# A transformer tower with an expert layer on one core: where small weights, zero rows and a slot table are made, and in which order the middle stage issues its parts

## The chip, the cores and the metric

One Trainium2 chip, one core of it. The time is the device time of one execution, in microseconds (us); the figure for a kernel is the median of its runs. A core has five engines that run their own instruction streams and meet at semaphores: PE (TensorE, matrix products), DVE (VectorE), ACT (ScalarE), POOL (GpSimd) and SP (SyncE, which here only issues DMAs). A stream is executed strictly in order, so an instruction that waits holds up all that stands behind it on its engine. That goes for the queue of DMAs that an engine issues as well.

## The reference

The input is 128 images of 2x104x104. They become 128 x 169 = 21,632 tokens of 128 numbers (a patch embedding over five shifted copies of the image). Four residual blocks follow:

```python
h = _L0_tok_ref(x, gamma, beta, W, b)                       # patch embedding
h = h + _L0_attn_ref(_layernorm(h), positions, scales, ...)  # attention to 256 learned positions
h = h + _L0_ffn_ref(_layernorm(h), weight)                   # quantised product 128x128
h = h + _L1_attn_ref(_layernorm(h))                          # softmax(x x^T) x within an image
h = h + _L1_ffn_ref(_layernorm(h), ...)                      # 64 experts, six a token
```

The last one routes every token to six of 64 experts, adds a shared expert of all tokens, and has a capacity per expert of C = int(N * 6 * 2 / 64) rows:

```python
router_probs = softmax(x @ router_w.T + bias);  topk_p, topk_i = top_k(router_probs, 6)
slot = pos - group_starts                      # place of a pair within its expert
expert_in[e, slot] = x[token]                  # scatter
expert_out = (silu(expert_in @ w_gate.T) * (expert_in @ w_up.T)) @ w_down.T
sparse = segment_sum(gate * expert_out, token) # back to the tokens, six rows each
out = shared_out + sparse
```

## The kernel before

The program has three stages.

**Front** (to about 648 us): embedding and first attention, image positions in 43 groups of four. The change leaves it alone.

**Middle**: 64 blocks of two images (the b parts: quantised product and second attention) and 43 groups of four tiles of 128 tokens (the r parts: shared expert, routing, slots). All five engines walk through the same steps, in which a function `braid` (line 130) puts the parts. A part `('b', 1, scores)` stands in step s for block s-1; an r part has its group by `place_of(r) = LATE + 3*(r//2) + 2*(r%2)` (line 125), with LATE = 5. So from step 5 on, two steps of three carry an r group and the third has b parts alone. The order of the parts within a step is the order in the list, one list for each engine:

- PE (lines 1374 to 1377): shared_up, turn_q, ffn, turn_x, scores, count, shared_down, mix, turn_r, route.
- ACT (line 1495): tanh, norm_q, root_x, root_r, copy_q, copy_x, probs, expo, copy_x4.
- DVE (line 1837): ffn_out, silu_gate, quant, stats_r, root_x, root_r, norm_x, attn_out, choose, silu_up, place, denominator, norm, shared_out.

One block's chain is norm_q (ACT, L1415 and L1420), quant (DVE, L1522 to L1532), turn_q (PE, L1213), copy_q (ACT, L1391), ffn (PE, L1220), ffn_out (DVE, L1538, L1504, L1509), root_x (ACT L1428, then DVE L1516), norm_x (DVE, L1546), turn_x (PE, L1228), copy_x (ACT, L1398), scores (PE, L1238), expo (ACT, L1408), mix (PE, L1249), attn_out (DVE, L1555, L1561). One group's chain is stats_r, root_r (L1435, L1573), norm (L1580), turn_r (L1257), copy_x4 (L1452), route (L1268, L1271), then in the next r step tanh (L1459), silu_gate (L1616), shared_up (L1278), choose (L1593 to L1610), probs (L1466, L1471), silu_up (L1624), count (L1290, L1293), place (L1631 to L1652), denominator (L1660 to L1673), shared_down, shared_out (L1683).

POOL has one part, `scatter` (lines 1075 to 1090): after place and denominator of a group it issues 24 indirect DMAs, one for each tile and each of the six choices, which write 128 rows of `xr` into the list of the experts' rows `xed`. Behind each stands a one-column memset of `pace`, for which the next one waits.

SP issues load_h1, store_h3, store_h4 and load_h3 by the same steps. ACT's queue issues seven loads before its first step (lines 1437 to 1446): the router's and the shared expert's weights (rwt, sgu, sdt, rbias), the experts' weights for all 64 experts in two DMAs (wgu, 4096 KB, and wdt, 2048 KB), and the zero rows behind `xed`. The slot table `first` (the number of each expert's first row) is made in three steps: DVE writes a diagonal `diag`, PE multiplies ones by it (first_rows, line 1338, behind PE's parts of step 2), DVE copies the product (line 1715, in constants(), ahead of its parts of step 3).

After the middle, DVE and PE build tables of tiles (`tab_ready`). Then comes the **expert stage**: 270 steps q of four tiles. SP loads four row tiles (`xin<-xed`, L1150) whose numbers it reads from the table; PE turns and multiplies; ACT writes the weighted rows `yo` (L1491); POOL's `spread` (lines 1092 to 1103) issues four indirect DMAs a step, which write them to `ytk`, by token and choice. SP's DMAs that zero the ends of the experts' lists (lines 1180 to 1185) stand as one block between the loads of step q = 7 and q = 8. From q = 218 on a function `weave` adds one `add_up` (lines 1848 to 1871) in every second step, until 26 groups are done: SP loads 128x4x6 rows of 128 (`yg<-ytk`), DVE adds the six of each token, the first of its additions in one instruction on 128x1536 (L1856). Groups 26 to 31 follow behind the last step; the last eleven (32 to 42) wait until all spreads have landed.

## Time and profile before

| | us |
|---|---|
| median of three runs (lowest to highest) | 3638.26 (3630.31 to 3639.31) |
| the profiled execution | 3652.29 |
| its span in the trace | 3650.5 |
| front, to the first instructions of the middle | 648 |
| first scatter to last scatter on POOL | 785.6 to 2130.8 |
| spreads on POOL | 2131.1 to 3582.9 |
| from there to the end of the span | 67.6 |

Busy shares of the whole span are PE 72%, DVE 62%, ACT 44%, POOL 76%. A share over the span mixes the stages. The row of POOL in forty slices shows it at 8 and 9 tenths from slice 9 to slice 39. The other engines' rows stand well under theirs there. The granted TensorE clock is low (5 and 6 tenths of full speed) in the middle stage and 7 to 8 tenths in most of the expert stage. Register and branch instructions and the issuing of DMAs do not count as busy.

### The profile page before, as it was taken

The page shows a single profiled execution, that of the slowest core. Times are in us where ns is not written, and L with a number is a line of the kernel's source. Part 1 is how long each engine was busy: PE and PEld are TensorE (multiplying, and loading weights), DVE is VectorE, ACT ScalarE, POOL GpSimd, SP SyncE. Part 2 cuts the span into 40 slices and gives each one's busy share as a digit, 9 for nine tenths or more (in the row PEclk, how much of TensorE's full clock was granted, in tenths as well). Part 3 has the DMA queues.
Part 4 walks back from the last instruction along what each step waited for, and adds up shares of the span by engine and source line. Part 5 has one row for each costly group of instructions (what it writes and reads, how often), then busy time and mean ns, then how long its engine had stood idle before and what let it go on. Part 6 is the DMA issues. An engine that isn't in the chain of part 4 may idle for free. (4 is left out here: it accounts for less than half of the span.)

```text
span 3650.5 us, 70832 instructions
## 1 busy us (share of the span) xinstructions
PE 2639.7 (72%) x14073; PEld 1949.1 (53%) x14074; DVE 2248.0 (62%) x7707; ACT 1602.5 (44%) x4279; POOL 2765.1 (76%) x4608
## 2 busy tenths in 40 slices
PE   5888987477776777777677446777778888877770
PEld 4777775244443444444344245656667677667660
DVE  6999998466666667666666534444444444457665
ACT  4888887344443444444443123333333333333320
POOL 4777773038888888888888868888888888888882
PEclk7999998556656555655656569888887777777765
DMA  7777773313232222222222154334333333369768
GB/s 274 245 241 241 240 244 131 92 47 98 86 96 88 93 89 83 90 75 84 75 79 70 58 143 117 108 109 111 107 109 111 108 107 101 104 207 283 235 220 299
DMA packets 387802, 501.76 MB, mean 137 GB/s; under 512 B 68888, under 2 KB 319889, under 8 KB 376178
## 3 DMA queue, kind: packets, MB, share of 16 engines
q1 hardware_dynamic: 303458, 366.96, 33.3%
q0 software_dynamic: 83232, 126.60, 10.4%
q10 hardware_dynamic: 944, 6.63, 0.6%
q14 instruction: 144, 1.18, 0.1%
q8 instruction: 24, 0.39, 0.0%
HBM read 257.02 MB, written 264.08 MB: 143 GB/s over the span
## 5 line engine op out<-in xcount | busy, mean ns | idle before, releaser
L1097 POOL DMA_INDIRECT ytk<-yo,idxy x1080 | 1084.9, 1005 | 243.6 <-POOL pace L1103 204.1
L1085 POOL DMA_INDIRECT xed<-xr,idxs x1014 | 1002.9, 989 | 334.8 <-POOL pace L1090 176.2
L1491 ACT ACTIVATE yo<-wide,gi 128x128 f32<-128x128 f32 x1080 | 308.7, 368 | 894.1 <-DMA ytk<-yo,idxy 854.8
L1825 DVE SCALAR_TENSOR_TENSOR ae<-the,bank 128x256 f32<-128x256 f32 x270 | 113.5, 421 | 693.6 <-ACT the L1482 686.1
L1316 PE MATMUL bank<-wgu,xeT 128*128 x2160 | 392.5, 339 | 174.9 <-ACT xeT L1476 158.1
L1316 PEld LDWEIGHTS bank<-wgu,xeT 128*128 128x128 f32 x2160 | 347.0, 244 | 228.8 <-issue 228.1
L1334 PE MATMUL wide<-wdt,hT 64*128 x2160 | 373.4, 322 | 123.1 <-DVE hT L1834 121.5
L1334 PEld LDWEIGHTS wide<-wdt,hT 64*128 64x128 f32 x2160 | 312.8, 220 | 175.7 <-issue 173.0
L586 POOL TENSOR_TENSOR weff<-w,gam 128x384 f32<-128x384 f32 x338 | 305.4, 938 | 9.1 <-DMA tokb<-in_tokb 9.1
L1249 PE MATMUL wide<-xn,e 128*128 128x128 f32 (+3 forms) x1024 | 251.9, 366 | 43.2 <-ACT e L1408 43.2
L1306 PE MATMUL bank<-ident,xin 128*128 128x128 f32 x1080 | 214.1, 334 | 46.8 <-DMA xin<-xed 46.8
L1238 PE MATMUL bank<-xnT 128*128 128x169 f32 (+1 forms) x512 | 206.5, 532 | 41.9 <-ACT xnT L1398 41.9
L597 POOL TENSOR_TENSOR big<-big,scb 128x1024 f32<-128x1024 f32 (+1 forms) x43 | 103.9, 2416 | 171.7 <-ACT big L729 171.7
L1249 PEld LDWEIGHTS wide<-xn,e 128*128 128x128 f32 (+3 forms) x1024 | 144.3, 187 | 149.4 <-issue 74.1
L1325 PE MATMUL wide<-ident,hh 128*64 128x128 f32 x1080 | 217.5, 337 | 0.0
L1476 ACT ACTIVATE xeT<-bank 128x512 f32<-128x512 f32 x270 | 165.8, 614 | 85.8 <-PE bank L1306 85.7
L618 PE MATMUL bank<-weff,xs 128*128 128x128 f32 x1690 | 200.5, 279 | 0.8 <-POOL weff L586 0.8
L1306 PEld LDWEIGHTS bank<-ident,xin 128*128 128x128 f32 x1080 | 171.1, 177 | 53.1 <-issue 47.3
L618 PEld LDWEIGHTS bank<-weff,xs 128*128 128x128 f32 x1690 | 196.5, 196 | 2.6 <-issue 2.6
L1834 DVE COPY hT<-wide 64x512 f32<-64x512 f32 x270 | 182.6, 676 | 16.9 <-PE wide L1325 15.5
L1452 ACT ACTIVATE x4T<-wide 128x512 f32<-128x512 f32 (+1 forms) x43 | 25.4, 590 | 313.4 <-PE wide L1257 313.4
L1238 PEld LDWEIGHTS bank<-xnT 128*128 128x128 f32 (+1 forms) x512 | 91.7, 237 | 129.5 <-issue 113.0
(324 smaller groups left out, 5428.9 us busy)
## 6 DMA issues: line engine op xcount, KB each, us to landing
xin<-xed SPq DMA_DIRECT2D x1080, 74.0 KB
ytk<-zeros SPq DMA_DIRECT2D x42, 1536.0 KB, 9.6
yg<-ytk SPq DMA_DIRECT2D x42, 1536.0 KB
xs<-in_xcol SPq DMA_DIRECT2D x42, 1280.0 KB, 6.7
ytk<-yo,idxy POOLq DMA_INDIRECT x1080
xed<-xr,idxs POOLq DMA_INDIRECT x1014
H<-in_ximg SPq DMA_DIRECT2D x4, 2704.0 KB, 19.2
h1d<-H SPq DMA_DIRECT2D x42, 256.0 KB, 9.0
```

Of the source, the lines that this page charges most:

```text
L586: ins = p.tensor_tensor(weff[:, slot, j, k0:k1, :], w5[:, k0:k1, :], gam[:, bass.ds(TG * g + j, 1), k0:k1].rearrange("p o c -> p (o c)").u ...
L618: pe.matmul(psY[slot][:, j * D:(j + 1) * D], xs[:, slot, j, k, :], weff[:, slot, j, k, :], start=(j == 0 and k == 0), stop=False)
L1085: p.indirect_dma_start(xed[:, :], bass.IndirectOffsetOnAxis(ap=idxs[:, slot, j, k:k + 1], axis=0), xr[:, slot, j, :], None, bounds_check=Z ...
L1097: p.indirect_dma_start(ytk[:, :], bass.IndirectOffsetOnAxis(ap=idxy[:, slot, j:j + 1], axis=0), yo[:, slot % ES, j, :], None, bounds_check ...
L1238: last = pe.matmul(dst, xnT[:, i, 128 * h:128 * h + m], xnT[:, i, 0:T], start=True, stop=True)
L1249: last = pe.matmul(pP[0:m, 256 * i + D * h:256 * i + D * h + D], e[0:m2, i, 128 * h:128 * h + m], xn[0:m2, slot, 2 * i + h2_, :], start=(h ...
L1306: last = pe.transpose(eT_[slot % 2][:, j * 128:(j + 1) * 128], xin[:, slot, j, 0:D], ident[:, :])
L1316: last = pe.matmul(eG[slot % 2][:, j * 128:(j + 1) * 128], xeT[:, slot % 2, j, :], wgu[:, bass.ds(e, 1), :].rearrange("p o f -> p (o f)"), ...
L1325: last = pe.transpose(eH[slot % 2][0:F, j * 128:(j + 1) * 128], hh[:, slot % 2, j, :], ident[:, :])
L1334: last = pe.matmul(eO[slot % 2][:, j * D:(j + 1) * D], hT[:, slot % 2, j, :], wdt[:, bass.ds(e, 1), :].rearrange("p o f -> p (o f)"), star ...
L1491: last = a.activation(yo[:, slot % ES, j, :], eO[slot % 2][:, j * D:(j + 1) * D], ACT.Copy, scale=gi[:, slot, j, 0:1])
L1834: v.tensor_copy(hT[:, slot % 2, :, :].rearrange("p j d -> p (j d)"), eH[slot % 2][0:F, :])\
```

## The change

Four items and a new order of the middle stage.

1. The seven loads leave ACT's queue. SP issues load_h1 of blocks 0 and 1 first, then the small weights and the zero rows, and then its braid from step 2. The experts' weights come expert by expert: load_weights stands in the braid with lag 2 and issues two DMAs a block (64 KB and 32 KB). PE waits for all of them at the head of the expert stage.
2. The slot table comes from a POOL iota (1 + CR * e, the same in every partition) and one DVE copy. `diag`, first_rows and DVE's wait for it are gone, and PE's braid is one piece.
3. The DMA that zeroes an expert's tail is a part of the steps q = 8 to 71, one in each, behind the four row loads of that step.
4. The first addition of add_up is four instructions on 128x384 in place of one on 128x1536.
5. Order. Each engine's list of the middle stage changes. PE: turn_x moves ahead of turn_q, scores ahead of ffn. ACT: root_x goes first, copy_x moves ahead of root_r and copy_q. DVE: root_x, norm_x and attn_out move ahead of quant. One of the two PSUM places of turn_x moves from bank 0 to bank 3.

```diff
-    pX = (bank[0][:, 256:256 + T], bank[2][:, 2 * T:3 * T])
+    pX = (bank[3][:, 2 * T:3 * T], bank[2][:, 2 * T:3 * T])
...
+            p.iota(firsti[:, :], [[CR, NE]], base=1, channel_multiplier=0)
...
-            braid(sp, 0, place_of(GR + 2, LATE) + 1, LATE,
-                  [('b', 0, load_h1), ('b', 3, store_h3), ('r', 3, halves(store_h4)), ('r', 0, load_h3)], 0, GR)
+            def load_weights(g, slot, rnd):
+                sp.dma_start(wgu[:, bass.ds(g, 1), :], io["wgu"][:, bass.ds(g, 1), :]).then_inc(n["s_wt"], 16)
+                sp.dma_start(wdt[:, bass.ds(g, 1), :], io["wdt"][:, bass.ds(g, 1), :]).then_inc(n["s_wt"], 16)
+
+            load_h1(0, 0, 0)
+            load_h1(1, 1, 0)
+            for dst, src in ((rwt, io["rwt"]), (sgu, io["sgu"]), (sdt, io["sdt"])):
+                sp.dma_start(dst[:, :], src).then_inc(n["s_ws"], 16)
...
+            braid(sp, 2, place_of(GR + 2, LATE) + 1, LATE,
+                  [('b', 0, load_h1), ('b', 2, load_weights), ('b', 3, store_h3), ('r', 3, halves(store_h4)), ('r', 0, load_h3)], 0, GR)
...
-            for e in range(0, NE, 4):
-                for row in entries(SP, ttail, e, 4, ZR - 128):
-                    sp.dma_start(xed[bass.ds(row, 128), :], zrow[:, :]).then_inc(n["tail_z"], 16)
-            pipeline(sp, 0, NQ, rows, ES, begin=2 * ES, end=Q0)
+            def zero_tail(q, slot, rnd):
+                row, = entries(SP, ttail, q - 2 * ES, 1, ZR - 128)
+                sp.dma_start(xed[bass.ds(row, 128), :], zrow[:, :]).then_inc(n["tail_z"], 16)
+
+            pipeline(sp, 0, NQ, rows + [(0, zero_tail)], ES, begin=2 * ES, end=2 * ES + NE)
+            pipeline(sp, 0, NQ, rows, ES, begin=2 * ES + NE, end=Q0)
...
-            def first_rows():
-
-                pe.wait_ge(n["first_v"], 1)
-                pe.matmul(rB[:, 0:NE], ones[0:NE, :], diag[:, :], start=True, stop=True).then_inc(n["first_p"], 1)
...
-            parts = [('r', 1, halves(shared_up)), ('b', 0, turn_q), ('b', 0, ffn), ('b', 1, turn_x),
-                               ('b', 1, scores), ('r', 1, halves(count)), ('r', 1, halves(shared_down)), ('b', 1, mix),
+            parts = [('r', 1, halves(shared_up)), ('b', 1, turn_x), ('b', 0, turn_q), ('b', 1, scores),
+                               ('b', 0, ffn), ('r', 1, halves(count)), ('r', 1, halves(shared_down)), ('b', 1, mix),
                                ('r', 0, turn_r), ('r', 0, halves(route))]
...
-            a.wait_ge(h1_in[0], 32)
-            a.wait_ge(h1_in[1], 32)
-            a.dma_start(rwt[:, :], io["rwt"]).then_inc(n["s_ws"], 16)
...
-            braid(a, 0, WHOLE[1], LATE, [('r', 1, halves(tanh)), ('b', 0, norm_q), ('b', 1, root_x), ('r', 0, root_r), ('b', 0, copy_q),
-                              ('b', 1, copy_x), ('r', 1, probs), ('b', 1, expo), ('r', 0, halves(copy_x4))], 0, GR)
+            braid(a, 0, WHOLE[1], LATE, [('b', 1, root_x), ('r', 1, halves(tanh)), ('b', 0, norm_q), ('b', 1, copy_x), ('r', 0, root_r),
+                              ('b', 0, copy_q), ('r', 1, probs), ('b', 1, expo), ('r', 0, halves(copy_x4))], 0, GR)
...
-                v.tensor_scalar(diag[:, :], ident[0:C, 0:C], col[0:C, 10:11], None, ALU.mult).then_inc(n["first_v"], 1)
-                v.wait_ge(n["first_p"], 1)
-                link(v.tensor_copy(first1[:, :], rB[:, 0:NE]))
+                link(v.tensor_copy(first1[:, :], firsti[:, :]))
...
-            order = [('b', 1, ffn_out), ('r', 1, halves(silu_gate)), ('b', 0, quant), ('r', 0, stats_r), ('b', 1, root_x),
-                     ('r', 0, root_r), ('b', 1, norm_x), ('b', 2, attn_out), ('r', 1, choose), ('r', 1, halves(silu_up)),
+            order = [('b', 1, ffn_out), ('b', 1, root_x), ('b', 1, norm_x), ('r', 1, halves(silu_gate)), ('b', 2, attn_out),
+                     ('b', 0, quant), ('r', 0, stats_r), ('r', 0, root_r), ('r', 1, choose), ('r', 1, halves(silu_up)),
...
-                v.tensor_tensor(y[:, :, 0:3, :], y[:, :, 0:3, :], y[:, :, 3:6, :], ALU.add).then_inc(n["add1_r"], 1)
+                for j in range(nj):
+                    last = v.tensor_tensor(y[:, j, 0:3, :], y[:, j, 0:3, :], y[:, j, 3:6, :], ALU.add)
+                last.then_inc(n["add1_r"], 1)
```

In the program's order the change shows at three places. The first is ACT in a step with an r group. `th` is tanh's result, `mrs` and `xq` are norm_q's, `sdb` root_x's, `sdc` root_r's, `xqT` copy_q's, `xnT` copy_x's, `ex` that of probs. ACT_TABLE_LOAD fetches the table of the function that follows it. Before:

```order
L1459 ACTIVATE th<-wide 128x512
L1415 ACTIVATE mrs<-mur 128x8
L1420 ACTIVATE xq<-h1s,mrs 128x128 x4
L1428 ACT_TABLE_LOAD
L1428 ACTIVATE sdb<-mvc,eps_ln 128x4
L1435 ACTIVATE sdc<-mvd,eps_ln 128x4
L1391 ACTIVATE xqT<-bank 128x512
L1398 ACTIVATE xnT<-bank 128x169 x2
L1466 ACT_TABLE_LOAD
L1466 ACTIVATE ex,zz<-lo,top 128x64 x4
```

After, the same step (its lines are some four to seven lower or higher):

```order
L1435 ACT_TABLE_LOAD
L1435 ACTIVATE sdb<-mvc,eps_ln 128x4
L1455 ACT_TABLE_LOAD
L1455 ACTIVATE th<-wide 128x512
L1422 ACTIVATE mrs<-mur 128x8
L1427 ACTIVATE xq<-h1s,mrs 128x128 x4
L1405 ACTIVATE xnT<-bank 128x169 x2
L1442 ACT_TABLE_LOAD
L1442 ACTIVATE sdc<-mvd,eps_ln 128x4
L1398 ACTIVATE xqT<-bank 128x512
L1462 ACT_TABLE_LOAD
L1462 ACTIVATE ex,zz<-lo,top 128x64 x4
```

root_x went ahead of tanh and copy_x ahead of root_r, and the step has four table loads where it had two.

The second is DVE in the same step, from ffn_out's last instruction on. `xn` is norm_x's result, `sa` silu_gate's, `h` attn_out's in the rows with `rzb`, `xq` and `qmag` are quant's. Before:

```order
L1509 BN_AGGR mvc<-bstc 128x2 x4
L1616 SCALAR_TENSOR_TENSOR sa<-th,wide 128x512
L1522 TENSOR_SCALAR xq<-xq 128x512
L1524 TENSOR_SCALAR qmag<-xq 128x512
L1527 TENSOR_SCALAR qmag<-qmag 128x512
L1529 TENSOR_TENSOR xq<-xq,qmag 128x512
L1532 TENSOR_TENSOR xqb<-xq,qmag 128x512
L1504 BN_STATS bstd<-h3s 128x6 x4
L1509 BN_AGGR mvd<-bstd 128x2 x4
L1516 RECIPROCAL rb<-sdb 128x4
L1573 RECIPROCAL rc<-sdc 128x4
L1546 TENSOR_SCALAR xn<-h,mvc,rb 128x128 x4
```

After:

```order
L1505 BN_AGGR mvc<-bstc 128x2 x4
L1512 RECIPROCAL rb<-sdb 128x4
L1542 TENSOR_SCALAR xn<-h,mvc,rb 128x128 x4
L1612 SCALAR_TENSOR_TENSOR sa<-th,wide 128x512
L1551 RECIPROCAL rzb<-zsum 128x2
L1551 RECIPROCAL rzb<-zsum 41x2
L1557 SCALAR_TENSOR_TENSOR h<-wide,rzb,h 128x128
L1557 SCALAR_TENSOR_TENSOR h<-wide,rzb,h 41x128
L1557 SCALAR_TENSOR_TENSOR h<-wide,rzb,h 128x128
L1557 SCALAR_TENSOR_TENSOR h<-wide,rzb,h 41x128
L1518 TENSOR_SCALAR xq<-xq 128x512
```

The root and norm_x went ahead of silu_gate, attn_out ahead of quant.

The third is SP at the start of the middle stage, where `h1s` is what load_h1 fills. Before:

```order
L1113 DMA h1s<-h1d 128x2x128
L1114 DMA h1s<-h1d 41x2x128
L1113 DMA h1s<-h1d 128x2x128
L1114 DMA h1s<-h1d 41x2x128
L1113 DMA h1s<-h1d 128x2x128
L1114 DMA h1s<-h1d 41x2x128
```

After:

```order
L1151 DMA rbias<-in_rbias 128x64
L1153 DMA xed<-zrow 128x148
L1114 DMA h1s<-h1d 128x2x128
L1115 DMA h1s<-h1d 41x2x128
L1144 DMA wgu<-in_wgu 128x128
L1145 DMA wdt<-in_wdt 64x128
L1114 DMA h1s<-h1d 128x2x128
L1115 DMA h1s<-h1d 41x2x128
L1144 DMA wgu<-in_wgu 128x128
L1145 DMA wdt<-in_wdt 64x128
```

The small loads stand between those of block 1 and block 2, and each block's load is followed by the two for one expert's weights.

## Rows read from the trace of the kernel before

**Rows 1.** The page: busy time in forty slices, in tenths.

```profile
POOL 4777773038888888888888868888888888888882
```

**Rows 2.** Groups by line on POOL, 785.5 to 2131 us: busy, mean ns, idle before.

```profile
L1085 POOL DMA_INDIRECT xed<-xr,idxs x1014 | 1002.9, 989 | 334.8 <-POOL pace L1090 176.2 <-issue 145.8 <-DVE xr L1673 3.5
L1090 POOL MEMSET pace<- 128x1 f32 x1014 | 150.7, 149 | 0.0
```

**Rows 3.** The page, the group of the spreads, same columns.

```profile
L1097 POOL DMA_INDIRECT ytk<-yo,idxy x1080 | 1084.9, 1005 | 243.6 <-POOL pace L1103 204.1
```

**Rows 4.** Timeline of POOL at the first scatter: start, length, idle before it.

```profile
785.59 1.31 POOL L1085 DMA_INDIRECT xed<-xr,idxs  x1 [125.29 <-issue]
```

**Rows 5.** Waits of POOL, 785.5 to 2131 us: total, times, longest.

```profile
POOL xed L1085 <- DVE xr L1673: 3.5, 3, 1.4
```

**Rows 6.** Timeline of ACT at the head of the middle stage.

```profile
656.30 0.40 ACTq L1439 DMA_DIRECT2D rwt<-in_rwt  x1
...
659.89 0.21 ACT L1415 ACTIVATE mrs<-mur 128x8 f32<-128x8 f32 x1 [21.50 <-issue]
```

**Rows 7.** Waits of ACT, 640 to 790 us, and of DVE, 660 to 790 us.

```profile
ACT mrs L1415 <- DMA h1s<-h1d: 4.7, 1, 4.7
...
DVE first L1715 <- PE wide L1341: 10.0, 1, 10.0
```

**Rows 8.** Timeline of DVE, 1228 to 1358 us, single rows.

```profile
1228.98 0.17 DVE L1673 SCALAR_TENSOR_TENSOR xr<-e,rden 128x24 f32<-128x24 f32 x1
...
1236.75 0.69 DVE L1616 SCALAR_TENSOR_TENSOR sa<-th,wide 128x512 f32<-128x512 f32 x1 [3.92 <-issue]
...
1243.37 1.14 DVE L1546 TENSOR_SCALAR xn<-h,mvc,rb 128x128 f32<-128x128 f32 x4
...
1244.67 1.12 DVE L1561 SCALAR_TENSOR_TENSOR h<-wide,rzb,h 128x128 f32<-128x128 f32 x4
...
1251.08 0.42 DVE L1631 TENSOR_TENSOR slotm<-wide,taken 128x256 f32<-128x256 f32 x1 [2.33 <-PE wide L1293]
...
1357.17 0.17 DVE L1673 SCALAR_TENSOR_TENSOR xr<-e,rden 128x24 f32<-128x24 f32 x1
```

**Rows 9.** Timeline of ACT in and behind the same step.

```profile
1231.59 0.60 ACT L1452 ACTIVATE x4T<-wide 128x512 f32<-128x512 f32 x1 [7.13 <-PE wide L1257]
...
1238.46 1.28 ACT L1428 ACT_TABLE_LOAD   x1
1239.75 0.30 ACT L1428 ACTIVATE sdb<-mvc,eps_ln 128x4 f32<-128x4 f32 x1
...
1271.76 1.28 ACT L1408 ACT_TABLE_LOAD   x1 [3.46 <-PE bank L1238]
```

**Rows 10.** Timelines of POOL and SP around the only large gap.

```profile
2175.00 0.97 POOL L1097 DMA_INDIRECT ytk<-yo,idxy  x1 [17.87 <-issue]
...
2123.76 3.36 SPq L1185 DMA_DIRECT2D xed<-zrow  x6
...
2164.52 1.93 SPq L1150 DMA_DIRECT2D xin<-xed  x4
```

**Rows 11.** Timelines of POOL and DVE at two of the 32 additions beside spreads.

```profile
3274.84 2.03 POOL L1097 DMA_INDIRECT ytk<-yo,idxy  x1 [0.19 <-POOL pace L1103]
...
3286.17 2.49 POOL L1097 DMA_INDIRECT ytk<-yo,idxy  x1 [0.19 <-POOL pace L1103]
...
3274.27 1.75 DVE L1856 TENSOR_TENSOR yg<-yg 128x1536 f32<-128x1536 f32 x1
...
3286.05 1.76 DVE L1856 TENSOR_TENSOR yg<-yg 128x1536 f32<-128x1536 f32 x1
```

**Rows 12.** Timeline of DVE at the end; its waits, 3583 to 3650 us.

```profile
3643.27 1.76 DVE L1856 TENSOR_TENSOR yg<-yg 128x1536 f32<-128x1536 f32 x1 [2.38 <-DMA yg<-ytk]
...
3647.06 0.55 DVE L1856 TENSOR_TENSOR yg<-yg 128x384 f32<-128x384 f32 x1
...
DVE yg L1856 <- DMA yg<-ytk: 25.6, 10, 9.0
```

21 lines of the change are left out of this document (7 added, 14 removed).

## The prediction

> **What bounds the kernel now.** I read the busy rows in forty slices first [rows 1]: POOL stands at 8 or 9 tenths from slice 9 to slice 39, and no other engine does. Then POOL's groups. The 1014 scatters take 1002.9 us, their memsets 150.7, and the idle time ahead of them is 334.8, of which 125.3 lie before the first one [rows 2, 4]. The rest is the 0.2 us behind each memset, and some 20 us of "issue" in eight short pieces, where the loop returns. Only 3.5 us are a wait for DVE's last routing row [rows 5]. The 1080 spreads look the same: 1084.9 us busy and 243.6 idle, of which 204.1 are the short waits for the memset; of the remainder one piece is 17.87 us [rows 3, 10]. So from 785.6 to 3582.9 us POOL issues one indirect DMA behind the other at a pace of its own, and nothing that shortens other engines' work counts unless it (a) starts POOL earlier, (b) removes a wait of POOL, (c) makes one of its instructions shorter, or (d) shortens what lies behind its last one.
>
> The next question is how much room there is under POOL in the middle stage. 1014 scatters in 1345.2 us are 127.4 us for four groups (96 scatters). DVE's row for one group and the same row four groups later are 1228.98 and 1357.17, 128.2 us apart [rows 8]. The two are equal, so the middle has no reserve: POOL and the chain of the other engines are level.
>
> **The change part by part.**
>
> *Loads off ACT, start of the middle.* ACT's seven issues run from 656.30 until norm_q starts at 659.89 [rows 6]: 3.6 us, and ACT waited for both blocks' inputs first, of which it now needs one. I take 4.4. Behind them the two big loads fill the DMA engines, and norm_q of block 2 waited 4.7 us for its input [rows 7]; that goes. DVE waited 10.0 us for the slot table's product, because PE makes it behind all its parts of step 2 [rows 7]. The iota takes it away, but PE's and ACT's parts of the next steps are due soon after; part of the ten comes back there. Against this stand four or five steps without r groups before the first scatter, in which attn_out (1.12 us [rows 8], with its reciprocals 1.3) now lies ahead of quant: 1.1 to 1.5 us each. If all gains stay the sum is -4.4 - 4.7 - 10.0 + 5 = -14; if half of the ten comes back, -9. Laying the rows' durations on the queues in the new order by hand, wait by wait, gave the first scatter at about 772 instead of 785.6: **-13.6**, bounds -9 to -17.
>
> *Weights on SP.* 128 more issues, two a block, in a queue that is idle most of each step. An issue on a hardware queue takes about 0.5 us (656.30 to 659.89 holds seven [rows 6]), so 1.0 us a block against a step of 13 to 27 us. They stand behind load_h1 and ahead of store_h3 and load_h3, which are needed a step later: nothing. If SP were late it would show as "DMA h1s" or "DMA h3s" waits of ACT and DVE.
>
> *The order of the middle.* In a step with an r group DVE waits 3.92 us before silu_gate, then later 2.33 us before place, for PE's count, which stands behind scores [rows 8]. norm_x (1.14) and attn_out (1.3) move into or next to the first wait, and since turn_x and scores then start earlier, count is ready earlier. That is 2.4 + 1.7 = about 4.2 us off each r step, 16.8 off four groups; the two steps without r groups in the same span cost 1.1 to 1.5 each, +3. 128.2 - 16.8 + 3 = 114.4. Against it go eight more table loads in four groups, 1.28 each: 10.3 if all of them lie on the chain. Two of them in each r step are free where ACT waits anyway: behind copy_x4 it idles from 1232.2 until tanh's input comes at about 1236 [rows 9], room for root_x with both loads around it. The hand layout gave 22.3 and 23.4 us for the r steps, 14.4 for the others, so about 120 for four groups; with all loads on the chain it is 125. Both are under POOL's 127.4. Faster work under a full POOL gives only POOL's waits back: **-4**, bounds 0 to -6. The chain then runs ahead until the ring of four groups stops it.
>
> The load's price is 1.28 us, and the next function starts 0.01 us behind it [rows 9]. Eight of them are the 10.3 above.
>
> The Trainium skill ("ScalarE: Activation LUTs", "What ACT_TABLE_LOAD costs") adds a drain of 1380 ns to its 1283 ns, 2.66 us a switch. By that estimate the eight would be 21.3 us and four groups 114.4 + 21.3 = 135.7, above POOL's pace. The trace disagrees, with the 0.01 us between the load and the next function [rows 9], and I hold to the row.
>
> *Zero rows.* The only large gap of the spreads, 17.87 us at 2175.00, ends when the rows of q = 8 arrive; SP issued their loads at 2164.52, behind 64 zero DMAs that began at 2123.76 [rows 10]. With one a step SP needs per q four loads and a zero DMA, at 0.62 each (40.8 us over 64 with their register work [rows 10]) about 3.2 us, against 5.2 of POOL's four spreads. The loads run ahead, the gap goes: 17.87 - 0.19 = **-17.7**, bounds -14 to -17.8. Also, DVE and PE come to the tables earlier (the ring is four groups, so up to 28 us), and the first tiles with them.
>
> *The addition in pieces.* While DVE adds 128x1536 from SBUF, a spread that starts within it lasts 2.03 and 2.49 us instead of 0.97: the first ends 0.85 us behind the DVE instruction's end (3274.27 + 1.75 + 0.85 = 3276.87), the other too (3286.05 + 1.76 + 0.85 = 3288.66) [rows 11]. So POOL gets in when the DVE instruction is over. For a start anywhere within a period of 1.28 us the mean loss is 1.76 - 0.64 + 0.85 - 0.97 = 1.0 us, 32 us for the 32 additions beside spreads. With pieces of 0.55 us [rows 12] or a little less, it is at best 0.13 each time, and 0.2 to 0.5 with the pieces behind: a gain of 0.45 an addition, **-14**, bounds 0 to -20, if POOL gets in between pieces.
>
> *The tail.* The last eleven additions wait for `yg<-ytk`, 2.38 us in the row before the last [rows 12]. Four pieces of 0.55 take up to 0.44 us more than one of 1.76; ten of eleven times the wait takes it up, the last one pays: **+0.5**.
>
> **Sum.** -13.6 - 4 - 17.7 - 14 + 0.5 = -48.8. 3652.3 for the profiled execution becomes 3603.5. That execution lies 14 above the median of 3638.26; a change in microseconds carries over, so the median becomes 3589.5.
>
> **The rivals.**
>
> *Pieces give nothing.* The 2.03 and 2.49 us of the two spreads could have another cause than DVE's hold, say the DMA load of this stretch, and then cutting the instruction gives 0; or DVE keeps POOL out across all four pieces, and the longer sum of 2.2 us costs up to 0.44 each, 14 in all. What speaks against it: both rows end 0.85 behind DVE's end, at different lengths [rows 11]. The sum is then -35 to -21: median 3603 to 3617. A rule on a page points this way: the Trainium skill ("SBUF — State Buffer", "Who interferes with whom") has it that a tensor_tensor takes only the read interface of the pair shared with GpSimd, and infers that the making of descriptors needs the write interface. By that the addition wouldn't hold a spread up; the rows of the two spreads speak against it.
>
> *The middle chain falls behind POOL* (the slower side). Place: ACT in the r steps, with its four table loads. It costs from 127.4 us for four groups on, 10.6 us over the stage for each microsecond, and it outweighs the other gains (13.6 + 17.7 + 14 = 45) from 127.4 + 4.3 = 131.7 on. With all loads on the chain and half of the gain in waits lost it is 128.2 - 8.4 + 3 + 10.3 = 133.1, the middle ends 60 us later, and the median is 3638 - 45 + 60 = 3653. For it: POOL and the chain are level now, ACT, PE and DVE all get a new order, and one load of the three in the rows started only when its input was there (1271.76 [rows 9]). Against it: DVE alone waits 6.25 us in the r step shown [rows 8], and two of the new loads fall where ACT idles.
>
> *The start gives half.* The ten microseconds return as a wait for PE: 3594.
>
> *The change doesn't do what it says at the gap.* The loads of q = 8 wait for another thing (the ring of row tiles, or DVE's table work), and half of the 17.7 stays: 3598.
>
> **How the numbers follow.** The forecast (all terms within their bounds) 0.68; pieces without effect 0.12; half of the start or of the gap 0.10; the chain behind POOL 0.10, of which 0.04 end above 3649 and 0.04 within 11 us of the old median; another 0.01 of that last kind is in the others. The range goes from 3570, all terms at their better ends (-17 - 6 - 17.8 - 20 = -61, plus some spread of the median), to 3618, where pieces and start fail together. 0.3% is 11 us, about what a measurement of this kernel tells from no change. Faster 0.91, same 0.05, slower 0.04.
>
> **What would show it.** Right: the first scatter at 770 to 776; POOL's spacing in the middle 127 to 128 us for four groups with no "DVE xr" waits behind the first groups; DVE's and ACT's idle time in the middle now ends with waits for POOL's scatter (the ring) rather than with PE and ACT; no gap in spreads near the twentieth; spreads beside additions 1.0 to 1.6 us long. Wrong: POOL waits "<-DVE xr" once in each group, table loads that start behind a wait, spreads still over 2 us beside additions, or a new wait of PE for weights at the head of the expert stage.

## The result

The changed kernel takes 3595.47 us (median of four runs, 3594.43 to 3598.39), the kernel before 3635.39 us (four runs, 3630.31 to 3639.31). The ratio is 0.9892, 95% interval 0.9875 to 0.9909: 1.1% faster, about 40 us. The forecast was 3589.5 us, 48.8 less than before, in a range from 3570 to 3618. The direction was right, and three of the four gains came. Two terms had the wrong size, the start and the middle, and the middle's also the wrong sign; the gain at the gap came, and would have come without the edit that it was put down to.

The profiled execution of the changed kernel has a span of 3593.1 us. The page's row of POOL in forty slices and its two groups of indirect DMAs, which answer to [rows 1 to 3]:

```profile
POOL 5777773048888888888888888888888888888882
...
L1086 POOL DMA_INDIRECT xed<-xr,idxs x1014 | 1007.9, 994 | 314.0 <-POOL pace L1091 181.5
L1098 POOL DMA_INDIRECT ytk<-yo,idxy x1080 | 1068.9, 990 | 226.4 <-POOL pace L1104 204.6
```

POOL is as full as before. The scatters' idle time holds no wait for DVE any more, and the spreads' mean length fell from 1005 to 990 ns. The waits of POOL over the scatters (total, times, longest), which answer to [rows 5]:

```profile
POOL xed L1086 <- POOL pace L1091: 181.5, 899, 1.0
POOL xed L1086 <- issue: 127.4, 11, 105.3
```

The line "<-DVE xr" of before is gone. The timelines of SP and POOL at the start of the middle stage (start, length, idle time before it), SP's first load and POOL's first scatter, first SP's in the kernel before:

```profile
649.34 0.39 SPq L1113 DMA_DIRECT2D h1s<-h1d  x1
```

The timeline of SP in the changed kernel:

```profile
642.68 0.39 SPq L1114 DMA_DIRECT2D h1s<-h1d  x1
```

The timeline of POOL in the same kernel:

```profile
759.72 1.31 POOL L1086 DMA_INDIRECT xed<-xr,idxs  x1 [105.27 <-issue]
```

The first scatter came 117.0 us behind the first load. In the kernel before it was 136.2 (785.59 [rows 4] minus 649.34). The same two engines where the gap of [rows 10] was:

```profile
2058.40 23.20 SPq L1162 DMA_DIRECT2D xin<-xed  x36
2082.22 0.36 SPq L1197 DMA_DIRECT2D xed<-zrow  x1
2083.36 1.92 SPq L1162 DMA_DIRECT2D xin<-xed  x4
2086.21 0.37 SPq L1197 DMA_DIRECT2D xed<-zrow  x1
```

The timeline of POOL in the same kernel:

```profile
2134.25 0.97 POOL L1098 DMA_INDIRECT ytk<-yo,idxy  x1 [0.19 <-POOL pace L1104]
```

SP now goes from row loads to one zero DMA and back, and the twenty-first spread (2134.25) follows at the usual distance of 0.19 us.

So the two profiled executions divide like this:

| stretch | before | after | difference | forecast |
|---|---|---|---|---|
| front, to SP's first load of the middle | 649.3 | 642.7 | -6.7 | 0 |
| first load to first scatter | 136.2 | 117.0 | -19.2 | -13.6 |
| first to last scatter | 1345.2 | 1348.1 | +2.8 | -4 |
| spreads, with the gap | 1452.0 | 1418.0 | -34.1 | -17.7 - 14 |
| behind the last spread | 67.6 | 67.4 | -0.2 | +0.5 |
| span | 3650.5 | 3593.1 | -57.3 | -48.8 |

The pair of executions differs by 57 us and the medians by 40. The experiments say which part of the 57 is not the change.

### The profile page after: what moved, and what is told of

It reads as the page before. It is cut to its first block and busy times, and to the rows that moved or that the text cites. A ratio compares the mean times of both kernels' runs of the same rounds, so it can differ in the third digit from the quotient of the medians.

```text
span 3593.1 us, 71455 instructions
## 1 busy us (share of the span) xinstructions
PE 2624.0 (73%) x14071; PEld 1956.1 (54%) x14072; DVE 2257.3 (63%) x7831; ACT 1696.0 (47%) x4357; POOL 2751.8 (77%) x4609
## 3 DMA queue, kind: packets, MB, share of 16 engines
q0 software_dynamic: 83232, 126.60, 10.6%
## 5 line engine op out<-in xcount | busy, mean ns | idle before, releaser
L1098 POOL DMA_INDIRECT ytk<-yo,idxy x1080 | 1068.9, 990 | 226.4 <-POOL pace L1104 204.6
L1330 PE MATMUL bank<-wgu,xeT 128*128 x2160 | 375.1, 328 | 198.8 <-ACT xeT L1472 181.2
L1348 PE MATMUL wide<-wdt,hT 64*128 x2160 | 388.3, 332 | 152.9 <-DVE hT L1827 152.9
L1330 PEld LDWEIGHTS bank<-wgu,xeT 128*128 128x128 f32 x2160 | 334.0, 236 | 243.3 <-issue 242.9
L1348 PEld LDWEIGHTS wide<-wdt,hT 64*128 64x128 f32 x2160 | 328.4, 230 | 204.3 <-issue 201.0
L586 POOL TENSOR_TENSOR weff<-w,gam 128x384 f32<-128x384 f32 x338 | 305.2, 936 | 10.6 <-DMA tokb<-in_tokb 9.1
L1263 PE MATMUL wide<-xn,e 128*128 128x128 f32 (+3 forms) x1024 | 263.6, 379 | 30.1 <-ACT e L1415 30.1
L1320 PE MATMUL bank<-ident,xin 128*128 128x128 f32 x1080 | 204.5, 323 | 8.2 <-DMA xin<-xed 8.2
L1339 PE MATMUL wide<-ident,hh 128*64 128x128 f32 x1080 | 208.7, 326 | 0.0
L1320 PEld LDWEIGHTS bank<-ident,xin 128*128 128x128 f32 x1080 | 162.7, 170 | 13.3 <-issue 7.8
L665 PE MATMUL bank<-v,big 128*128 128x128 f32 x676 | 104.5, 319 | 61.3 <-DVE H L825 60.9
```

Source lines behind the costliest of these rows:

```text
L586: ins = p.tensor_tensor(weff[:, slot, j, k0:k1, :], w5[:, k0:k1, :], gam[:, bass.ds(TG * g + j, 1), k0:k1].rearrange("p o c -> p (o c)").u ...
L1098: p.indirect_dma_start(ytk[:, :], bass.IndirectOffsetOnAxis(ap=idxy[:, slot, j:j + 1], axis=0), yo[:, slot % ES, j, :], None, bounds_check ...
L1263: last = pe.matmul(pP[0:m, 256 * i + D * h:256 * i + D * h + D], e[0:m2, i, 128 * h:128 * h + m], xn[0:m2, slot, 2 * i + h2_, :], start=(h ...
L1320: last = pe.transpose(eT_[slot % 2][:, j * 128:(j + 1) * 128], xin[:, slot, j, 0:D], ident[:, :])
L1330: last = pe.matmul(eG[slot % 2][:, j * 128:(j + 1) * 128], xeT[:, slot % 2, j, :], wgu[:, bass.ds(e, 1), :].rearrange("p o f -> p (o f)"), ...
L1339: last = pe.transpose(eH[slot % 2][0:F, j * 128:(j + 1) * 128], hh[:, slot % 2, j, :], ident[:, :])
```

## The experiments

Runs were made on several chips. On two of them (those of the run with the weights alone and of the run that puts the zero DMAs back into a block) the kernel before takes 3636 to 3637 us, as in the result. On the other five, below called chips with pauses, it takes 4558 to 4647. What differs is visible in the first run below and changes what bounds the kernel there, so for those runs I use the traces' single stretches, and totals only beside the kernel before of the same chip. A DMA's "stretching" below is what it lasts beyond 0.97 us, summed over those that last about 0.1 us longer or more.

**The kernel before, once more.** No edit.

> The kernel before, once more. The two profiled executions put the first load of the middle stage at 649.3 us (before) and 642.7 us (after), although the front's code is the same, and the profiled execution of before is 17 us above its median. Theory 1: the front's length wanders by some 7 us from execution to execution; then this one's lies anywhere from 642 to 650 and from there to the first scatter it takes 136 us again, and the span is 3630 to 3650. Theory 2: something of the change reached the front; then 649 again. In both the gap of 17.9 us in the spreads comes back, and the 32 additions stretch spreads by 32 us.

It took 4656 us, and the median of the kernel before on this chip was 4647.28. POOL's timeline within the spreads:

```profile
2797.81 0.97 POOL L1097 DMA_INDIRECT ytk<-yo,idxy  x1 [3.87 <-ACT yo L1491]
...
2806.76 0.97 POOL L1097 DMA_INDIRECT ytk<-yo,idxy  x1 [0.19 <-POOL pace L1103]
2807.71 0.14 POOL L1103 MEMSET pace<- 128x1 f32 x1
2811.81 0.97 POOL L1097 DMA_INDIRECT ytk<-yo,idxy  x1 [3.96 <-issue]
```

The timeline of ACT in the same kernel:

```profile
2805.08 0.60 ACT L1476 ACTIVATE xeT<-bank 128x512 f32<-128x512 f32 x1 [4.05 <-issue]
...
2809.84 1.14 ACT L1491 ACTIVATE yo<-wide,gi 128x128 f32<-128x128 f32 x4
```

Every eight issues, 14 us apart, POOL stands still for some 3.9 us. The last row of POOL names no releaser, but the first names ACT's `yo`, and ACT's `yo` for the last one ends at 2810.98, 0.83 us before the spread starts. It is the same in each of the 127 steps here that POOL began over a microsecond late, and in the 125 to 133 such steps of every other trace from a chip with pauses: the first spread starts 0.83 to 0.85 us behind the end of its `yo`. In the profiled execution of the kernel before `yo` is ready 13.1 us (median) ahead of its spread. So on such a chip POOL isn't the bound of the spreads; it waits for the chain of the other engines. The 1.28 us between two issues are otherwise the same. In the middle DVE's rows of groups 0 and 1 are 27 us apart in the timeline of the kernel before (784.34 and 811.3) and 41 here (785.0 and 826.5), so there, too, the chain is slower and is the bound. ACT's idle time ahead of 2805.08 has no releaser in the profile. What slows the chain isn't settled.

The start doesn't suffer: 648.93 us to the first load and 137.3 from there to the first scatter, so the trace gives the start of all runs. The first load stands between 640.3 and 643.1 us in nine of the fourteen executions and between 648.7 and 649.8 in the other five, and the same kernel shows both (the new order alone 641.90 and 649.79, the version with both further edits 641.06 and 649.11). This run's 648.93 by itself would fit theory 2 as well; what decides for theory 1 is that one kernel shows both. The 6.7 us in the front are the execution's, not the change's. Taken off, the pair differs by 50.6 us.

**Each place by itself.**

The zero DMAs, one a step (item 3 alone):

```diff
-            for e in range(0, NE, 4):
-                for row in entries(SP, ttail, e, 4, ZR - 128):
...
+            def zero_tail(q, slot, rnd):
...
+            pipeline(sp, 0, NQ, rows + [(0, zero_tail)], ES, begin=2 * ES, end=2 * ES + NE)
```

> Only the zero DMAs one a step. Theory: the gap of 17.9 us in the spreads goes and nothing comes in its place, -17.7 us or -0.49%. Rival (another wait takes its place, as table work of DVE or the ring of row tiles): half of it or less, -9 to 0 us, with a new gap near the twentieth spread.

It ran on the chip with pauses: ratio 0.9973, interval 0.9937 to 1.0009, which settles nothing by itself. The trace does. In the kernel before on the same chip the twentieth spread is followed by a gap of 32.7 us from start to start; with this edit there is none. On a chip without pauses this edit wasn't run by itself.

The order of the middle alone, twice, on two chips (cut here to the PSUM place and the first line of DVE's list; PE's and ACT's lists change as above):

```diff
-    pX = (bank[0][:, 256:256 + T], bank[2][:, 2 * T:3 * T])
+    pX = (bank[3][:, 2 * T:3 * T], bank[2][:, 2 * T:3 * T])
...
+            order = [('b', 1, ffn_out), ('b', 1, root_x), ('b', 1, norm_x), ('r', 1, halves(silu_gate)), ('b', 2, attn_out),
```

> Only the new order of the middle stage (and the PSUM place that goes with it). Theory: POOL stays the bound of the middle, so the order itself gives 0 there: its waits of 3.5 us go, and scatters that DVE holds up cost some 7 us more (10.6 in before, 17.4 in after). But the chain ends early, the tables too, and then the 64 zero DMAs are issued before POOL needs q = 8: the gap of 17.9 us goes although they still stand as a block. At the start the steps without r groups are 1.1 to 1.5 us longer each, partly inside the 10 us wait for the slot table: +0 to +6. Sum -17.7 + 3.5 + 3 = -11, from -14 to -8. Rival A (the order shortens the path to the first scatter and so carries the 19 us seen there): first scatter 15 us or more earlier, sum -25 or below. Rival B (the gap belongs to the block of zero DMAs alone): gap stays, sum +3 to +10.

> Only the new order again, now where POOL has no pauses of its own (in the first run of it, as in the kernel before beside it, POOL stood still for about 4 us after every eleven issues and the total was 4600 us). From the first load of the middle stage to the first scatter 132.6 as there. Theory: scatters 1348 us in all instead of 1345 (waits of 3.5 us gone, some 7 us more of stretching), the tables start 20 us or more earlier, and the gap of 18 us goes though the zero DMAs still stand as a block; sum -4 + 3 - 17.7 = -19 us, -0.5%. Rival (the gap belongs to the block alone): gap of 15 us or more stays, sum 0 to -3.

Both runs were on chips with pauses (ratios 0.9973, 0.9937 to 1.001, and 0.9898, 0.9816 to 0.9981). The first scatter came 132.6 and 131.4 us behind the first load, against 137.3 for the kernel before on the first of these chips, so the order alone brings it 5 to 6 us earlier (4 to 6 over all executions with the old start), where the forecast had charged 5 for it. DVE held scatters up by 18.9 and 17.2 us, against 10.6 to 13.7 in the kernels with the old order: the extra stretching belongs to the order. The gap stayed. POOL and SP in the second of them:

```profile
2564.70 22.37 SPq L1150 DMA_DIRECT2D xin<-xed  x32
2589.91 44.17 SPq L1185 DMA_DIRECT2D xed<-zrow  x64
2634.91 25.40 SPq L1150 DMA_DIRECT2D xin<-xed  x25
```

The timeline of POOL in the same kernel:

```profile
2644.42 0.97 POOL L1097 DMA_INDIRECT ytk<-yo,idxy  x1 [30.67 <-issue]
```

SP issues the 64 zero DMAs for 44 us, and POOL waits 30.67 us. That would be the rival's case. But here the chain bounds the middle, and POOL has no backlog of scatters (work handed to it and not yet issued) with which to bridge the block. This is taken up by the run with the block put back, below.

The first addition in pieces alone:

```diff
-                v.tensor_tensor(y[:, :, 0:3, :], y[:, :, 0:3, :], y[:, :, 3:6, :], ALU.add).then_inc(n["add1_r"], 1)
+                for j in range(nj):
+                    last = v.tensor_tensor(y[:, j, 0:3, :], y[:, j, 0:3, :], y[:, j, 3:6, :], ALU.add)
+                last.then_inc(n["add1_r"], 1)
```

> Only the first addition in four pieces. Theory: the spreads that start in it last 0.2 to 0.5 us longer instead of 1.0, -13.6 us (32.2 us of stretching in before, 18.5 in after), -0.37%. Rival (a spread's length has to do with DMA load, not with DVE's instruction): 0, and the long spreads stay over 2 us.

The total says nothing on this chip (ratio 1.0008, 0.9967 to 1.0048): where POOL waits for ACT, a shorter spread is lost in the noise. The spreads' stretching is 18.2 us, and 28.1 in the kernel before on the same chip. Five executions with the whole addition, beside the profiled one's 32.2, show 27.4 to 29.6; five with pieces, and nothing else in add_up changed, show 15.8 to 20.1. So the piece is worth some 10 us and the profiled execution of before had 4 more than usual.

The weights alone, on a chip without pauses:

```diff
+            braid(sp, 2, place_of(GR + 2, LATE) + 1, LATE,
+                  [('b', 0, load_h1), ('b', 2, load_weights), ('b', 3, store_h3), ('r', 3, halves(store_h4)), ('r', 0, load_h3)], 0, GR)
...
-            a.wait_ge(h1_in[0], 32)
-            a.wait_ge(h1_in[1], 32)
-            a.dma_start(rwt[:, :], io["rwt"]).then_inc(n["s_ws"], 16)
```

> Only the weights moved to SP's queue, in before's order and with before's slot table. From the first load of the middle stage to the first scatter it takes 136.2 to 137.3 us in all runs of before's start, 132.6 with the new order alone, 117.0 with everything. Theory: ACT starts norm_q some 4 us earlier and block 2's input is not late (4.7 us), so 128 to 131; the wait for the slot table stays at about 10 us. Rival (the whole 19 us are due to the DMA queues being free): 120 or less. After the first scatter nothing changes, total -6 to -9 us.

3627.65 us against 3637.11, ratio 0.9978 (0.9967 to 0.9989), 4 to 12 us by the interval. POOL's first scatter and its gap, ACT's first step, and DVE's wait for the slot table (the wait's columns are total, times, longest):

```profile
766.31 1.31 POOL L1085 DMA_INDIRECT xed<-xr,idxs  x1 [114.94 <-issue]
...
2147.51 0.97 POOL L1097 DMA_INDIRECT ytk<-yo,idxy  x1 [9.31 <-issue]
```

The timeline of ACT in the same kernel:

```profile
644.94 0.21 ACT L1426 ACTIVATE mrs<-mur 128x8 f32<-128x8 f32 x1 [15.38 <-DMA h1s<-h1d]
```

The waits of DVE (total, times, longest) in the same kernel:

```profile
DVE first L1715 <- PE wide L1352: 10.5, 1, 10.5
```

With the first load at 640.50 the first scatter is 125.8 us behind it, 10.4 less than before; the expectation had 128 to 131, and the forecast 4.4 and 4.7. ACT's first step comes 4.4 us behind the load instead of 10.6 (659.89 [rows 6] minus 649.34). The wait for the slot table is untouched at 10.5. The gap has shrunk from 17.87 to 9.31 us although nothing of the zero DMAs changed. That was not expected. The two places make 19 us in the trace, and the totals differ by 9.5; the profiled execution, 3619.19, was the fastest of ten.

**The gap and the backlog.** The changed kernel with the zero DMAs in one block again:

```diff
-            pipeline(sp, 0, NQ, rows + [(0, zero_tail)], ES, begin=2 * ES, end=2 * ES + NE)
...
+            for e in range(0, NE, 4):
+                for row in entries(SP, ttail, e, 4, ZR - 128):
+                    sp.dma_start(xed[bass.ds(row, 128), :], zrow[:, :]).then_inc(n["tail_z"], 16)
...
```

> The changed kernel with the 64 zero DMAs in one block again. In the kernel before the gap at the twentieth spread is 17.7 us, and from DVE's last routing row to the last scatter it is 71.1 us; with the weights moved alone the two are 9.1 and 79.0. Their sum is 88.8 and 88.1: POOL's backlog covers the block as far as it reaches. In the changed kernel the backlog is 91.8. Theory: so the gap is gone there even with the block, where POOL is the bound (3595, the same as the changed kernel), and the order of the middle had already paid for it. On a chip whose engines pause, where the chain and not POOL sets the middle, the backlog is 34 us and the gap is 30 us or more, as in the other kernels with the block. Rival (the gap belongs to the block whatever the backlog is): 17 us of gap, 3612.

3593.46 us on a chip without pauses, ratio 0.9885 (0.9864 to 0.9907), the same as the changed kernel's. SP and POOL at the place:

```profile
2055.14 20.53 SPq L1162 DMA_DIRECT2D xin<-xed  x32
2076.30 40.52 SPq L1197 DMA_DIRECT2D xed<-zrow  x64
2117.66 7.19 SPq L1162 DMA_DIRECT2D xin<-xed  x12
```

The timeline of POOL in the same kernel:

```profile
2130.97 0.97 POOL L1098 DMA_INDIRECT ytk<-yo,idxy  x1 [0.19 <-POOL pace L1104]
```

The block stands there for 40.5 us, the loads of q = 8 leave at 2117.66, and no spread waits. The theory holds where it was run. What counts is the time from DVE's last routing row to POOL's last scatter, 71.1 us in the kernel before, 79.0 with the weights moved, 91.8 in the changed kernel and 91.7 here; the loads of q = 8 are late by 88.8 minus that, or not at all. The 88.8 is worked out from two executions (71.1 + 17.7, and 88.1 from 79.0 + 9.1). This kernel leaves out item 3 and has items 1, 2 and 5, so the three together take the gap on such a chip. Of the 20.6 us by which the backlog grew, 7.9 came with the weights; the order and the slot table weren't run apart here. That the order alone would do it isn't shown.

**What holds the scatters up.** quant ahead of attn_out in DVE's list, everything else as changed:

```diff
-            order = [('b', 1, ffn_out), ('b', 1, root_x), ('b', 1, norm_x), ('r', 1, halves(silu_gate)), ('b', 2, attn_out),
-                     ('b', 0, quant), ('r', 0, stats_r), ('r', 0, root_r), ('r', 1, choose), ('r', 1, halves(silu_up)),
+            order = [('b', 1, ffn_out), ('b', 1, root_x), ('b', 1, norm_x), ('r', 1, halves(silu_gate)), ('b', 0, quant),
+                     ('b', 2, attn_out), ('r', 0, stats_r), ('r', 0, root_r), ('r', 1, choose), ('r', 1, halves(silu_up)),
```

> The changed kernel with DVE's list turned at one place: quant ahead of attn_out again (root_x and norm_x stay ahead of silu_gate). In the changed kernel quant's first instruction follows attn_out's last and holds up 23 scatters by 9.9 us in all; in the kernel before it was 12 by 1.8. Theory (the collision comes from DVE's instruction standing ready directly behind attn_out): those go down to about 2, the scatters take 1341 instead of 1348 us, the total falls by 5 to 8 us to about 3589, since the chain has over 60 us of reserve at the end. Rival (the phases only shift, another DVE instruction collides in its place): 17 us of stretching as before, total within 2 us of 3595.

On a chip with pauses: ratio 0.9873 (0.9793 to 0.9953), so the forecast total is neither confirmed nor refuted. The stretching of scatters fell from 17.3 (14.1 in a further execution of the changed kernel on such a chip) to 11.8 us, and of that quant's first instruction has 2.3 instead of 9.9 and 8.4. Part of the rival holds too: quant's last instruction now collides 12 times, for 6.1 us. POOL's first scatter:

```profile
750.46 1.31 POOL L1086 DMA_INDIRECT xed<-xr,idxs  x1 [98.89 <-issue]
```

It is 109.9 us behind the first load (640.57), 7 us earlier than in the changed kernel, which I had not expected: the steps without r groups take 11.8 us instead of 14.4.

**Both together, and the change beside it.** In addition the three other additions of add_up in four pieces each (one of the three is shown):

```diff
-                v.tensor_tensor(y[:, :, 0, :], y[:, :, 0, :], y[:, :, 1, :], ALU.add).then_inc(n["add2_r"], 1)
+                for j in range(nj):
+                    last = v.tensor_tensor(y[:, j, 0, :], y[:, j, 0, :], y[:, j, 1, :], ALU.add)
+                last.then_inc(n["add2_r"], 1)
```

> The changed kernel with two edits: quant ahead of attn_out in DVE's list, and add_up's other three additions (128x512) in four pieces of 128x128 each as well. From the run with quant first alone: 109.9 us from the first load of the middle stage to the first scatter (117.0 in the changed kernel) and 11.8 us of stretched scatters (17.3), so -12.6. In the changed kernel the three other additions hold up spreads by 10.3 us in all and the pieces of the first by 8.3. Theory: in pieces of 0.3 us the three cost 3 us at most, so -7, and DVE's longer work (0.5 us an add_up) lies beside POOL; total 3595 - 12.6 - 7 = 3576, from 3572 to 3582. Rival (a piece costs DVE a start of its own and the pieces together hit as many spreads): -12.6 + 0 to 3, 3583 to 3586.

> The version of the run before once more, with quant ahead of attn_out and all of add_up's additions in four pieces; the change itself beside it for the direct comparison. Its first run gave 110.5 us to the first scatter, 13.4 us of stretched scatters and 12.5 of stretched spreads. Theory: the same again, and against the changed kernel -6.5 at the start, -4 in the scatters and -6 in the spreads, 16 us less or 0.45%. Rival (off the chip whose POOL has no pauses, nothing of it can be measured): the two within their noise, but the traces' three figures stand.

> The version with quant ahead of attn_out and all of add_up's additions in four pieces, a third time. Its two profiled executions gave 110.5 and 110.1 us to the first scatter against 117.0 to 119.3 in the changed kernel, 13.4 and 12.9 us of stretched scatters against 17.3, 12.5 and 10.8 us of stretched spreads against 18.5. Where POOL is the bound, theory: -7 - 4 - 7 = -18 against the changed kernel's 3595, so 3577, a ratio to before of 0.984. Rival (the phases of POOL and DVE shift and give part of it back): 3585 or more, 0.986 or more. On a chip whose engines pause: 0.985 to 0.987 again, as in the two runs before.

> The changed kernel once more, on the same chip as the version with the two further edits. In its profiled execution the start took 117.0 us, scatters were stretched by 17.3 us and spreads by 18.5. Theory: the same figures within 1 us at the start and 3 us in the other two, and the gap near the twentieth spread absent. Rival (those figures were one execution's luck): the start above 120 or the stretching of scatters back at 11.

All four ran on chips with pauses. The version's ratios are 0.9869 (0.9828 to 0.9911), 0.9848 (0.9805 to 0.989) and 0.9894 (0.9859 to 0.993); the change's own is 0.9851 (0.9792 to 0.9911). 4495.35 and 4495.01 us on the same chip are no difference. The change's own start, 119.3 us, missed its expectation of 117.0 within 1 us, and its scatters' stretching, 14.1 against 17.3, missed by a little; neither fell back to the values of before. The traces show the three single effects: 110.5, 110.1 and 110.3 us to the first scatter against 119.3, scatters stretched by 13.4, 12.9 and 12.2 us against 14.1, spreads by 12.5, 10.8 and 11.5 against 20.1. Together that is some 18 us of POOL's path. Where POOL is the bound it should show in the total, but no run was made there, so that this version beats the change is argued and not shown.

## Why the prediction was right, and where it wasn't

**POOL as the bound, and the reserve.** Right. The reading of the busy rows was too simple: slice 23 of POOL's row (counted from 0) is a 6, which is the gap, and PE's row stands at 8, as high as POOL's, in five slices of the expert stage. What makes POOL the bound are its waits, which name almost nothing but its own memset [rows 2, 3, 5]. The steps came out as laid by hand. DVE's rows of a group and of the same group four later in the changed kernel, which answer to [rows 8]:

```profile
1115.45 0.17 DVE L1669 SCALAR_TENSOR_TENSOR xr<-e,rden 128x24 f32<-128x24 f32 x1
...
1236.66 0.17 DVE L1669 SCALAR_TENSOR_TENSOR xr<-e,rden 128x24 f32<-128x24 f32 x1
```

121.2 us for four groups, forecast 120. A step without r groups takes 14.4 us: DVE's ffn_out stands at 665.31, 679.74 and 694.05 in its timeline. POOL takes 128 us for the four, so the backlog grew, from about 1690 us on the ring stopped DVE, and POOL's waits for DVE went to zero. The table loads did what was said of them. ACT in one r step:

```profile
1118.78 0.60 ACT L1448 ACTIVATE x4T<-wide 128x512 f32<-128x512 f32 x1 [7.71 <-PE wide L1271]
1119.39 1.28 ACT L1435 ACT_TABLE_LOAD   x1
1120.69 0.30 ACT L1435 ACTIVATE sdb<-mvc,eps_ln 128x4 f32<-128x4 f32 x1
1121.01 1.28 ACT L1455 ACT_TABLE_LOAD   x1
1123.25 0.60 ACT L1455 ACTIVATE th<-wide 128x512 f32<-128x512 f32 x1 [0.96 <-PE wide L1285]
...
1128.40 1.28 ACT L1442 ACT_TABLE_LOAD   x1
...
1130.72 1.28 ACT L1462 ACT_TABLE_LOAD   x1
1132.02 0.35 ACT L1462 ACTIVATE ex<-lo,top 128x64 f32<-128x64 f32 x1
```

The loads at 1119.39 and 1121.01 lie between copy_x4 and the arrival of tanh's input; tanh still waits 0.96 us for PE behind them. Those at 1128.40 and 1130.72 lie on the chain, and the reserve pays for them. The next function starts 0.01 to 0.02 us behind each load, where nothing else is waited for, and with 121.2 us for four groups the rival of the slower side didn't come. The drain of 1380 ns that the Trainium skill ("ScalarE: Activation LUTs", "What ACT_TABLE_LOAD costs") adds to a load isn't in these rows. The ring, and a price that the forecast left out, show in DVE's waits from 800 to 2000 us (total, times, longest):

```profile
DVE rb L1512 <- ACT sdb L1435: 71.2, 53, 1.8
...
DVE xr L1576 <- DMA xed<-xr,idxs: 40.0, 6, 11.5
```

The second row is the wait for POOL's scatters, named beforehand as the sign of the reserve; most of DVE's idle time still ends with PE and ACT. DVE waits for root_x in 53 steps, 71 us in all, since norm_x now stands right behind ffn_out. It is in the 121.2, and POOL doesn't see it.

**The start, -13.6.** Right in kind, too small: -19.2 in the profiled pair, outside the bound of -17, and 136.2 to 137.3 against 117.0 to 119.3 over the executions. The term "-4.4 - 4.7" measured 10.4. The step that failed is the balance of the other parts. The sum charged +5 for four or five steps without r groups and gave the new order no gain ahead of the first scatter. But the first group goes through r steps before it is scattered. In DVE's timeline the last interval of ffn_out before the first scatter was 27.0 us (759.02 to 786.05) in the kernel before and is 20.6 (739.61 to 760.19) in the changed one. The order alone is therefore -4 to -6, not +5. The remaining 3 to 5 us would be the slot table's by difference, if the three add up, against 10 in the forecast's best case and 5 in its other; the table alone wasn't run. The miss of 6 us is smaller than that of the order's term (9 to 11) only because the table was overrated.

**The middle, -4.** Wrong in sign and outside its bounds (0 to -6): +2.8, and +1.8 with the block of zero DMAs. The waits of 3.5 us went as forecast, but the step left out that DVE's instructions are also what stretches POOL's. The forecast had used this for the additions alone, where the rows were large. In the scatters it was 10.6 us before and is 17.3 now, of which quant's first instruction has 9.9 in 23 cases instead of 1.8 in 12. One of them, in POOL's and DVE's timelines:

```profile
1085.44 1.56 POOL L1086 DMA_INDIRECT xed<-xr,idxs  x1 [0.19 <-POOL pace L1091]
```

The timeline of DVE in the same kernel:

```profile
1084.70 1.12 DVE L1557 SCALAR_TENSOR_TENSOR h<-wide,rzb,h 128x128 f32<-128x128 f32 x4
1085.74 0.41 DVE L1518 TENSOR_SCALAR xq<-xq 128x512 f32<-128x512 f32 x1
```

The scatter started at 1085.44 while DVE was in attn_out's pieces, which read PSUM; quant's 0.41 us began 0.30 later, and the scatter ended at 1087.00, again 0.85 us behind DVE's end (1086.15). In the kernel before DVE reached quant from silu_gate or from the statistics, mostly out of a wait. That makes the difference: of the scatters that started up to 0.45 us ahead of quant's first instruction, it held 17 of 23 in the changed kernel, where it follows attn_out directly, and none of 15 in the kernel before. Why it can hold a scatter that started first isn't known; the run with quant ahead of attn_out takes these cases away (2.3 us left).

**The gap, -17.7.** The size was right and the cause half right. The prediction gave the gain to the zero DMAs' new place. Where POOL is the bound it would have come without that edit, by the backlog that items 1, 2 and 5 together build up (3593.46 us with the block, 3595.47 without). The prediction mentions the earlier tables, but in an afterthought, and didn't see that they make the edit redundant. On the chips with pauses, where there is no backlog, the zero DMAs' place is worth 30 us and more, and the order doesn't take the gap.

**The pieces, -14.** Right: stretching fell from 32.2 to 18.5 us, 13.6, of which the kernel before's execution had some 4 by luck, so 10, and the match with -14 is in part luck. Of the rest 8.3 belong to the pieces and 10.2 to the three other additions. Two spreads beside an add_up, POOL's and DVE's timelines, which answer to [rows 11]:

```profile
3208.73 1.17 POOL L1098 DMA_INDIRECT ytk<-yo,idxy  x1 [0.19 <-POOL pace L1104]
...
3210.20 1.49 POOL L1098 DMA_INDIRECT ytk<-yo,idxy  x1 [0.19 <-POOL pace L1104]
```

The timeline of DVE in the same kernel:

```profile
3207.57 1.95 DVE L1850 TENSOR_TENSOR yg<-yg 128x384 f32<-128x384 f32 x4
3209.56 0.69 DVE L1853 TENSOR_TENSOR yg<-yg 128x512 f32<-128x512 f32 x1
3210.17 0.68 DVE L1861 TENSOR_TENSOR yg<-yg,h3s 128x512 f32<-128x512 f32 x1
```

The four pieces run from 3207.57 to 3209.52. The first spread starts within the third, which ends at 3209.06, and lasts 1.17 us, not 2: it ends at 3209.90, again 0.85 behind that piece, and doesn't wait for the fourth. So POOL gets in between two pieces. The second spread is held by one of the 0.7 us additions and lasts 1.49. In the kernel before 54 spreads have the whole addition over them. The 31 that started when it had run for 0.05 us or more all ended 0.84 to 0.85 us behind it; of the other 23, which started before it or within 0.01 us of its start, 22 lasted 0.97 to 0.99 us. So it is the addition that DVE is already running which holds a spread, as the prediction's estimate assumed. The rival "pieces give nothing" is refuted: cutting the instruction alone took 10 us off. The Trainium skill ("SBUF — State Buffer", "Who interferes with whom") infers that a tensor_tensor leaves the making of descriptors alone; the spreads' lengths here disagree. The remaining 2.7 us of the spreads' 34.1 are their pace, 1.276 instead of 1.279 us from issue to issue, over 1080 of them.

**The tail, +0.5.** It was -0.2: the wait for `yg<-ytk` takes the pieces' time up.

**The total.** The forecast's method, to add the terms to the profiled execution and carry the difference to the median, has a fault of its own: that execution was 17 us above the later median. 6.7 of it lay in the front and 4 in the stretching of spreads. With both taken off the pair differs by some 47 us, and the medians by 40 (33 to 45 by the ratio's interval). The few that remain are open, as are those of the run with the weights alone, where the trace has 19 us less at two places and the totals 9.5.

**The signs named beforehand.** The first scatter came at 759.7 us, earlier than the 770 to 776 named, 6.7 of it by the front. Four groups took POOL 127.6 us on average, as named, without waits for DVE. The ring shows, but only six times. The gap is gone, and all but one of the stretched spreads last 1.5 us or less. Of the signs of being wrong one appeared: 14 table loads from 800 to 2000 us start behind a wait (29.3 us in all), which POOL doesn't see.

## What to carry to other kernels

When one engine is full, other engines' order counts only through what it does to that engine: when it starts, what it waits for, and which of its instructions get stretched. Ask of an order that frees time elsewhere which instruction will now stand next to the bound engine's, and count the stretched ones before and after. A gap that a backlog could bridge is not a term of its own: with the backlog there, the edit made for the gap was worth nothing. And a wait that the profile puts down to "issue" can still be one for another engine: look for the instruction that ends just ahead of it, every time.

## What was not expected of the hardware

- On five of seven chips the kernel before takes 4558 to 4647 us instead of 3636, and the same instructions of POOL take as long as elsewhere (0.97 us, 1.28 from issue to issue). The chain of the other engines is slower there, in the middle and in the expert stage, and POOL waits for ACT's `yo`, 3.9 us every 14. The front, to 640 to 650 us, is as fast as elsewhere. The cause is open.
- The front ends at 640.3 to 643.1 us or at 648.7 to 649.8, with nothing between, for the same code.
- A POOL indirect DMA that starts while DVE is adding two SBUF inputs ends 0.85 us behind DVE's end (3276.87 behind 3276.02; 31 of 31 for the whole addition, 31 of 31 for its pieces in the changed kernel). A DMA that starts first isn't held (one was, by 0.01 us), with the exception of quant's first instruction directly behind attn_out (1087.00 behind 1086.15, where DVE started 0.3 us after it). One-input instructions differ: quant's first, on 128x512, held 10 of 10 in the kernel before, norm_x's, on 128x128, 1 of 27 in the changed one. `hT<-wide`, which reads PSUM, held none of 62.
